# Swapping the two score blocks at the head of each TensorE step in an attention and mixture-of-experts kernel

## What is computed

```python
wq = (q @ wq_w.T + wq_b).reshape(b, t, H, DH)      # q: the layer norm of x
wk = (k @ wk_w.T + wk_b).reshape(b, t, H, DH)      # k, v: the context
wv = (v @ wv_w.T + wv_b).reshape(b, t, H, DH)
scores = jnp.einsum('bthd,bshd->bhts', wq, wk) / jnp.sqrt(jnp.float32(DH))
probs = jax.nn.softmax(scores, axis=-1)
attn = jnp.einsum('bhts,bshd->bthd', probs, wv).reshape(b, t, d)
x = x + (attn @ wo_w.T + wo_b)
x = x + ffn(layernorm(x))                          # 8 experts, the best one for each token
```

## Time and profile before

| | |
|---|---|
| median of 3 runs | 1657.25 us (1656.13 to 1658.98) |
| the profiled execution's own time | 1660.59 us |
| its span | 1658.5 us |
| granted TensorE clock, mean | 0.981 |
| DVE busy | 1209.4 us, 73% |
| ACT busy | 924.1 us, 56% |
| POOL busy | 424.1 us, 26% |

### The profile page before, as it was taken

One profiled execution on the slowest core, in us unless ns is written; L12 is line 12 of the kernel. 1 busy time (PEld: TensorE's weight loads), 2 busy tenths in 40 slices (PEclk: granted clock), 3 DMA queues, 4 the chain that ended last, 5 costly groups with the idle time before them and its releaser, 6 DMA issues.

```text
span 1658.5 us, 40318 instructions
## 1 busy us (share of the span) xinstructions
PE 1530.9 (92%) x15566; PEld 1225.0 (74%) x15566; DVE 1209.4 (73%) x2880; ACT 924.1 (56%) x1578; POOL 424.1 (26%) x600
## 2 busy tenths in 40 slices
PE   5899989999999999999999999968999999999998
PEld 4777777777777777777777777746777777777776
DVE  3688787777777777777777777655777777777775
ACT  4566766667667766776677666633233333333242
POOL 3222222222222222222222222201323222232321
PEclk8899999999999999999999999987999999999999
DMA  6455644555455545554555455411122121212121
GB/s 165 119 143 154 174 135 129 148 147 155 126 148 154 153 126 148 151 156 125 149 152 154 125 148 147 124 40 51 57 72 66 62 77 52 77 52 77 52 77 39
DMA packets 150742, 190.96 MB, mean 115 GB/s; under 512 B 17887, under 2 KB 101402, under 8 KB 150554
## 3 DMA queue, kind: packets, MB, share of 16 engines
q1 hardware_dynamic: 150554, 188.38, 40.7%
HBM read 53.01 MB, written 33.55 MB: 52 GB/s over the span
## 4 chain that ended last, share of the span: by engine, by line
PE 73%; DVE 16%; issue 5%; ACT 4%; DMA 1%; POOL 0%; SPq 0%; ACTq 0%; DVEq 0%; POOLq 0%
PE s_ps L510 12%; PE st_ps L528 12%; PE pp_ps L1203 8%; DVE negmax L927 8%; PE pv_ps L1149 6%; PE s_ps L1106 6%; PE pp_ps L1211 6%; PE pp_ps L1176 4%; PE st_ps L1134 3%; PE pv_ps L1157 3%; PE t_ps L1125 2%; PE pp_ps L476 2%; PE s_ps L517 2%; PE t_ps L1117 2%; PE pp_ps L1197 1%
## 5 line engine op out<-in xcount | busy, mean ns | idle before, releaser
L927 DVE TENSOR_REDUCE negmax<-s_ps 128x8 f32<-128x1024 f32 x256 | 313.2, 1223 | 137.3 <-PE s_ps L1106 129.4
L819 ACT ACTIVATE pT<-st_ps 128x1024 f32<-128x1024 f32 x256 | 263.0, 1027 | 102.8 <-PE st_ps L1134 102.5
L528 PE MATMUL st_ps<-w_hi,q_packed 128*128 128x256 f32 x1024 | 213.7, 294 | 0.7 <-DVE q_packed L430 0.7
L725 POOL TENSOR_TENSOR q_parts<-q,q_parts 128x1024 bf16<-128x1024 f32 x32 | 68.3, 2133 | 520.5 <-ACT q_parts L813 520.5
L1149 PE MATMUL pv_ps<-pT,v 128*32 128x128 f32 x4096 | 167.2, 279 | 27.6 <-DVE attn L943 18.9
L510 PE MATMUL s_ps<-k_packed,w_hi 128*128 128x512 f32 x512 | 174.2, 422 | 18.0 <-ACT pT L339 18.0
L528 PEld LDWEIGHTS st_ps<-w_hi,q_packed 128*128 128x128 f32 x1024 | 168.0, 188 | 10.4 <-issue 6.4
L333 ACT ACTIVATE offhotT<-pv_ps 96x512 bf16<-96x512 bf16 x32 | 19.0, 593 | 257.8 <-PE pv_ps L497 257.8
L1134 PE MATMUL st_ps<-q_packed,k_packed 98*128 98x128 bf16 x2048 | 158.6, 220 | 4.0 <-DMA q_packed<-negmaxT 3.1
L1106 PE MATMUL s_ps<-k_packed,q_packed 96*128 96x128 bf16 x2048 | 158.6, 220 | 2.5 <-DVE negmax L927 1.3
L1106 PEld LDWEIGHTS s_ps<-k_packed,q_packed 96*128 96x128 bf16 x2048 | 128.4, 98 | 25.1 <-issue 21.4
(11 more groups left out here) (165 smaller groups left out, 3626.5 us busy)
## 6 DMA issues: line engine op xcount, KB each, us to landing
q_packed<-q_parts SPq DMA_DIRECT2D x192, 256.0 KB, 3.8
k_packed<-k_parts SPq DMA_DIRECT2D x192, 256.0 KB, 4.2
xin<-in_x_dram SPq DMA_DIRECT2D x32, 512.0 KB, 3.6
cin<-in_ctx_dram SPq DMA_DIRECT2D x32, 512.0 KB, 3.6
x_scratch<-xb SPq DMA_DIRECT2D x32, 512.0 KB, 5.1
xin<-x_scratch SPq DMA_DIRECT2D x32, 512.0 KB, 4.6
out_dram<-xb SPq DMA_DIRECT2D x32, 512.0 KB, 3.2
q_packed<-negmaxT SPq DMA_DIRECT2D x256, 4.0 KB
```

Of the source, the lines that this page charges most:

```text
L528: t.matmul(o, h[n % 2][:, m, tok].bitcast(F32R), w[:, m, :].bitcast(F32R), start=(m == 0 and k == 0), stop=False)
L725: g.tensor_tensor(parts[z][:, 2, :, :], z32[z][:], parts[z][:, 1, :, :], ALU.subtract).then_inc(s_lo, 1)
L819: a.activation(pT[u % 2][:], st_ps[:], ACT.Exp, scale=DH ** -0.5).then_inc(s_exp, 1)
L927: v.tensor_reduce(negmax[u % 2][:], s_ps[:].rearrange("p (h s) -> p h s", s=P), AX_X, ALU.max, negate=True).then_inc(s_red, 1)
```

## The change

In both kinds of step, `scoresT` of the step's own unit moves ahead of `scores` of the unit two ahead. Nothing else is changed: the same matmuls, waits and signals, and the lists of all other engines as they were.

```diff
             def even(n, u):
                 nxt, done, before = later(n, u, 2), turned_at(n, u), later(n, u, -1)
+                scoresT(n, u)
                 if nxt:
                     scores(*nxt)
-                scoresT(n, u)
                 items(n, u, slice(0, 1))
...
             def odd(n, u):
                 nxt, done = later(n, u, 2), turned_at(n, u)
+                scoresT(n, u)
                 if nxt:
                     scores(*nxt)
-                scoresT(n, u)
                 if done:
                     turn_pv(*done)
```

## The result

| | before | after |
|---|---|---|
| median | 1656.84 us (4 runs) | 1761.89 us (4 runs, 1759.25 to 1764.38) |
| profiled execution's own time | 1660.59 us | 1760.09 us |
| span | 1658.5 us | 1758.2 us |
| granted clock, mean | 0.981 | 0.976 |

A forecast was written before the change was run, and what follows sets the result against it. PE was taken to wait on DVE's chain behind the maxima, which start 0.45 us later each step; less slack, 3.10 us a group, 97.4 us in all with the ends, gave 1755 us (+5.9%), range 1718 to 1785.

The forecast's parts named there:

- step 4: Fifth of a group's 8 steps (0 to 7): DVE's `aT_lo` has 0.06 us of slack before PE's load; costs 0.37 us.
- step 0: First step of a group: `remainder` stands ahead of the maxima and doesn't move; costs 0.24 us.
- step 7: Last step of a group: `values` starts 0.58 us after `attn`, slack taken as 0.06; costs 0.39 us.
- Step 5: Sixth step of a group: `values` waits for `attn`, whose operations meet POOL's pieces; costs 0.10 to 0.57 us, taken as 0.30.
- The row of maxima: Row that `scoresT` needs in step 5, loaded by DMA: there in time; where later, a wait up to some 0.4 us.
- `exp`'s gain counted at nothing: All steps: `exp` may start 0.45 us earlier on ACT, but PE and DVE don't wait for the copies behind it.
- The ends: Groups 0, 30 and 31, outside the steady groups: 1.5 us for group 0, 1.96 plus 4.05 us for 30 and 31.
- the rival on the clock: Longer stalls in steps 5 and 6 lower TensorE's clock once a group: 47 us on top, 1802 us; chance 0.06.
- steady term: Groups 1 to 29 at 3.10 us each, the sum of the eight step prices: 89.9 us.
- Hidden slack: Rival: only steps with recorded waits (0, 1, 2, 5, 6) pay, 1.65 us a group: 1712 us; chance 0.12.
- Faster: Rival: earlier `exp` frees ACT's copies, PE gets back 0.39 us a group through `uvT`: 1645 us; chance 0.03.
- nothing: Rival: same matmuls on a busy engine and all chains with slack, so no change: 1657 us; chance 0.03.

The follow-up runs named there:

- e8: Kernel before, with `scoresT` of steps 0, 2 and 6 put behind the step's first item, so `exp` starts later and the maxima stay: 1679.9 us (1.014).

## Why the prediction was right

- **What bounds the kernel.** It said that a busy PE (92%) does not make its order indifferent, since both consumers wait for it and only DVE's result is waited for in the same step. Right, and shown three ways: the waits of after, the step that gets longer wherever it is swapped, and `stats`.
- **The price of a step.** 0.45 less slack, step by step. Seven of eight terms hold to 0.06. The slack was read well in step 4 (0.06 said, 0.05 measured), the price in step 0 (0.24 said, 0.23 measured); the slack was taken too high in step 7: it has none, 0.45 was paid where 0.39 was said.
- **Step 5** was the mis-sized term: 0.30 taken, 0.14 measured. The 0.10 worked out for the group shown would have been nearer. The spread around it came from POOL, as said (4.5 to 5.4 in the groups of after; 4.35 to 4.42 with POOL held), but part of the low price is the bound behind it, the wait at the head of step 6, which the prediction didn't name.
- **The row of maxima.** Said to be there in time because steps 3 and 4 put T off. Right: 18 waits in 25.6 groups, 0.2 us each, in the kernel after, 26 of 0.5 us in 26.7 groups where step 4 isn't swapped.
- **`exp`'s gain counted at nothing.** Right: ACT's 82.9 us of waiting vanished and no step got shorter by it. The reason given was too wide: the copies behind `exp` are waited for as soon as they come 0.44 us later in step 6, where ACT and DVE end together.
- **The ends.** 7.5 us were given to groups 0, 30 and 31; they and the start cost 14.2. Group 31 alone cost 7.2 instead of 2.7. That is the rival on the clock, in the one place where it came true beyond the kernel before. The windows of after, in the columns of the earlier trace rows, without items:

```profile
1162.00:1166.00 4.00, 1.33 (x16) 0.93 (x18) 3.17 (x5) 1.08 (x2) 2.76 (x4) 0.78 0.28 73
1166.00:1170.00 4.00, 4.00 (x49) 2.94 (x39) 0.98 (x1) 1.40 (x2) 0.00 (x0) 0.50 0.02 5
...
1178.00:1182.00 4.00, 2.54 (x39) 1.97 (x39) 2.17 (x6) 1.78 (x3) 0.00 (x0) 1.00 0.02 5
...
1186.00:1190.00 4.00, 2.91 (x26) 2.01 (x26) 2.31 (x5) 0.51 (x2) 0.00 (x0) 0.50 0.00 0
```

Steps 0 and 1 of group 31, at 1.00 or 2.4 GHz, took 4.14 and 4.31 us. From 1182 to 1184 us PE was busy 0.66 of 2 us; from 1184 us on the granted clock was 0.50 to 0.81, a mixture of 1.2 and 2.4 GHz, and steps 2 to 6 took 5.2 to 5.8 us. In the kernel before it was 1.00 from 1082 to 1098 us and 0.91 from there to 1112, with steps of 3.7 to 3.9 us but for the last. The steady groups kept 1.00 (120 to 1050 us), as the prediction argued. Too high a steady term (89.9 against 86.2) and too low ends met, so that 97.4 in the sum stands against 99.7 in the spans: part of the closeness is luck. The medians are 105 us apart, because the profiled execution of after is one of its faster ones and that of before one of its slower.

- **The signs it named.** The period is 36.3 us, the maxima start at T + 1.10 in the step shown, the clock stays at 1.00. But PE's waits for `attn`, `aT_lo` and `xb` rose from 1.5 to 3.6 us a group, not from 2 to some 5. PE also waits for `negmax_p` ahead of `turn_max` in step 5, 0.7 us in each group, which was not named; `values` behind it waits for `attn` in any case.
- **A slip.** The group followed is 33.13 us long (403.42 to 436.55), not 33.17; only the argument on the clock uses it, and it stands.
- **The rivals.** Hidden slack fell with steps 3, 4 and 7, which recorded no wait on PE and paid 0.40 to 0.45. "Faster" and "nothing" fell with the time; e8 bounds what lies in `exp`. The price of 1802 us for the clock was not reached.

## What to carry to other kernels

When one engine feeds two others back to back, put first the block whose consumer's result the feeding engine needs again in the same step, even where the engine is 92% busy: here 0.45 us of order, less the slack, eight times a group, was 6.3%. See that the other consumer has the slack to come second: moved back, `exp` had over 1 us of it in two steps and none in a third. To price such a swap, write down for each step the distance from the awaited result to its use, and compare it with that distance in a step that is known to wait; a record without an idle time beside it may have no slack at all. The same reading finds gains: an operation that nobody needs yet (`stats`) in the middle of that chain was worth its full 0.34 us in each of four steps behind the swap, and in the kernel before 0.32 in two of them, where PE's recorded idle time was 0.25 and 0.29.

## What the runs showed of the hardware

A small DVE operation from SBUF to SBUF (128 x 8, 0.17 us) that meets GpSimd's running pieces is held to the end of a piece, and the next one to the end of the next. Step 5 of group 30 in the kernel after:

```profile
1162.01 2.76 POOL L733 TENSOR_TENSOR xb<-xin,bo_all 128x256 f32<-128x256 f32 x4 [4.64 <-DMA x_scratch<-xb]
1162.14 1.23 DVE L927 TENSOR_REDUCE negmax<-s_ps 128x8 f32<-128x1024 f32 x1 [1.17 <-PE s_ps L1106]
...
1163.40 0.71 DVE L932 TENSOR_TENSOR negmax_p<-negmax 128x8 bf16<-128x8 f32 x1
1164.15 0.65 DVE L934 TENSOR_TENSOR negmax_p<-negmax,negmax_p 128x8 bf16<-128x8 f32 x1
```

The four pieces end at some 1162.70, 1163.39, 1164.08 and 1164.77 (2.76 in four, an estimate), and the two operations at 1164.11 and 1164.80. L927, whose input is in PSUM, runs beside POOL at its usual 1.23. With POOL held off, both small operations are 167 ns in the mean, as shown above. The Trainium skill (SBUF — State Buffer, "SBUF: two separate sides") gives this, for a DVE operation with two SBUF inputs against one of GpSimd that reads SBUF, as an exclusive lock on a shared port pair, held for a whole instruction; the rows agree.

The granted clock was 1.00 from 1178 to 1182 us in group 31, with PE busy 2.54 of 4 us, and 0.50 from 1186 to 1190 with 2.91, where the matmuls were already the slower ones. In the kernel before, the stretch from 1084 us on, with PE busy 2.89 of 4 us, stayed at 1.00. What makes the difference is not shown.

The last packing DMA, issued 1.97 us earlier, landed 0.10 us earlier, as told above: in this queue the place of one issue brought next to nothing.
